# A start of its own for the first two batches: stacks copied inside SBUF, second-layer weights on other engines, an earlier output projection

## What is computed

```python
x = x + _L0_attn_ref(_layernorm(x), Wq, bq, Wk, bk, Wv, bv, Wo, bo)
x = x + _L0_ffn_ref(_layernorm(x), gamma, beta, fc1_q, fc1_scales, fc1_bias, fc2_q, fc2_scales, fc2_bias)
# attention: q = elu(x @ Wq.T + bq) + 1, k the same with Wk, v = x @ Wv.T + bv, in chunks of 128 tokens:
scores = where(mask, einsum('bqd,bkd->bqk', qi, ki), 0)
num = einsum('bqk,bkd->bqd', scores, vi) + einsum('bqd,bde->bqe', qi, S)
den = sum(qi * (cumsum(ki) + z)); out = num / den        # S += ki.T @ vi, z += sum(ki)
# then out @ Wo.T + bo
# feed-forward: w = (q - 128) * scales (groups of 128 rows), h = layernorm(x) * gamma + beta
y = silu(h @ w1 + fc1_bias); z = y @ w2 + fc2_bias; out = residual + 0.5 * z
```

## Time and profile before

| | |
|---|---|
| median of 3 runs | 1519.85 us |
| profiled execution | 1522.6 us |
| its span, first to last instruction | 1520.8 us |
| TensorE busy | 1493.2 us (98%) |
| VectorE busy | 1283.5 us (84%) |
| ScalarE busy | 1129.7 us (74%) |
| GpSimd busy | 680.7 us (45%) |
| mean granted TensorE clock | 0.991 |

### The profile page before, as it was taken

The page is one execution under the profiler, slowest core; times in us unless marked ns, Lnnn a source line. Parts: engine busy times, 40 slices in busy tenths (PEclk is TensorE's granted clock), DMA queues, the critical chain, the costliest instruction groups (busy, mean ns, idle before and its releaser), DMA issues.

```text
span 1520.8 us, 40737 instructions
## 1 busy us (share of the span) xinstructions
PE 1493.2 (98%) x14874; PEld 1311.2 (86%) x14874; DVE 1283.5 (84%) x2587; ACT 1129.7 (74%) x1917; POOL 680.7 (45%) x469
## 2 busy tenths in 40 slices
PE   7799999999999999999999999999999999999998
PEld 6588889888888888888888888888888888988887
DVE  6788888888888888888888888888888888888875
ACT  3487777887777887777887777887777877777863
POOL 3244344544344544345444445443445443445444
PEclk8899999999999999999999999999999999999999
DMA  7846765556765556764557765557654557755450
GB/s 198 194 118 150 179 148 149 137 131 152 179 158 131 131 133 164 179 156 133 131 122 175 179 133 143 137 125 179 179 138 138 133 129 179 174 134 141 117 127 28
DMA packets 153944, 222.96 MB, mean 147 GB/s; under 512 B 20032, under 2 KB 71488, under 8 KB 153920
## 3 DMA queue, kind: packets, MB, share of 16 engines
q1 hardware_dynamic: 152560, 222.63, 61.0%
q10 hardware_dynamic: 1360, 0.01, 0.1%
HBM read 138.69 MB, written 83.89 MB: 146 GB/s over the span
## 4 chain that ended last, share of the span: by engine, by line
PE 93%; DVE 2%; DMA 2%; POOL 1%; issue 1%; SPq 0%; ACT 0%; POOLq 0%; DVEq 0%
PE ring L342 35%; PE num L532 8%; PE ring L420 8%; PE sc L490 7%; PE ring L421 7%; PE sc L342 6%; PE num L499 4%; PE num L342 3%; PE state_acc L342 3%; PE ring L372 3%; PE state_acc L490 2%; PE ring L566 2%; PE state_acc L513 2%; PE num L421 1%; PE num L420 1%; PE num L372 1%
## 5 line engine op out<-in xcount | busy, mean ns | idle before, releaser
L1137 POOL TENSOR_TENSOR s_lo<-silu_f,s_hi 128x512 fp32r<-128x512 f32 x256 | 343.9, 1349 | 539.0 <-ACT s_hi L987 538.9
L342 PE MATMUL ring<-w_hi,s_hi 128*128 128x256 f32 x992 | 282.2, 284 | 0.0
L342 PE MATMUL ring<-w_lo,s_hi 128*128 128x256 f32 x992 | 278.9, 281 | 0.0
L342 PE MATMUL ring<-w_hi,s_lo 128*128 128x256 f32 x992 | 278.9, 281 | 0.0
L672 DVE TENSOR_TENSOR probs<-sc,causal 128x512 f32<-128x512 f32 x320 | 207.6, 681 | 16.1 <-PE sc L490 8.6
L342 PEld LDWEIGHTS ring<-w_hi,s_hi 128*128 128x128 f32 x992 | 187.8, 189 | 12.1 <-DVE phi_q L718 12.0
L1032 ACT ACTIVATE x_hat<-x,hn_add,ln_rstd 128x256 f32<-128x256 f32 x128 | 66.5, 590 | 174.6 <-DVE hn_add L860 174.6
L976 ACT ACTIVATE silu_f<-ring,bias,scale 128x512 f32<-128x512 f32 x217 | 167.5, 772 | 31.9 <-PE ring L421 23.5
L420 PE MATMUL ring<-gt_hi,w_q 128*128 128x512 f32 x441 | 190.5, 432 | 0.0
L342 PEld LDWEIGHTS ring<-w_hi,s_lo 128*128 128x128 f32 x992 | 188.0, 189 | 0.0
L342 PEld LDWEIGHTS ring<-w_lo,s_hi 128*128 128x128 f32 x992 | 187.9, 189 | 0.0
(11 more groups left out here) (204 smaller groups left out, 3946.2 us busy)
## 6 DMA issues: line engine op xcount, KB each, us to landing
k_stack<-k_rows SPq DMA_DIRECT2D x192, 256.0 KB, 4.1
q_stack<-q_rows SPq DMA_DIRECT2D x384, 128.0 KB, 6.2
k_rows<-silu_f SPq DMA_DIRECT2D x128, 256.0 KB, 2.6
q_rows<-probs SPq DMA_DIRECT2D x128, 256.0 KB, 2.5
x_in<-in_x SPq DMA_DIRECT2D x32, 512.0 KB, 8.4
xb<-in_x SPq DMA_DIRECT2D x32, 512.0 KB, 7.9
out<-clip SPq DMA_DIRECT2D x64, 256.0 KB, 7.5
silu_f<-in_q SPq DMA_DIRECT2D x2, 512.0 KB, 10.4
```

Source lines behind the costliest of these rows:

```text
L342: last = e.matmul(target, a, b, start=(n == 0), stop=(n == 3 * len(pairs) - 1))
L1137: sl.done(e.tensor_tensor(s_lo[:, j, :], silu_f[:, j % SLOTS, :], s_hi[:, j, :].bitcast(F32), ALU.subtract))
```

## The change

It touches the preparation and iterations 0 and 1, which is now unrolled as well (flag `second`); the loop begins at 2 and its order is as before.

- First stacks (batch 0): keys are copied from SBUF to SBUF by `first_keys`, 12 copies of 64 KB for each tile; SP issues those of tile 0, ScalarE those of tile 1. Queries still go over DRAM, those of tile 0 in two halves of the tokens. In iteration 0 SP does the same with the keys of tile 0 for batch 1 (`sp_second_stacks`), the others as before but in another order.
- Masked scores of batches 0 and 1 take the tiles in the order `FIRST_TILE`, which begins with the tiles that aren't `probs`.
- Second-layer weights: `fc2_q` is loaded at the start into x1 and res, the scales into `silu_f` once the key stacks are there; ScalarE casts, GpSimd multiplies and subtracts, ScalarE makes the high parts earlier.
- Iteration 0: TensorE does `output_projection` ahead of `project_kq(1)`; VectorE does `attention_sum` ahead of features(2) and features(3), and the small vectors' work (`ffn_preparation`) ahead of features(0); GpSimd adds `bias_o` and takes the power ahead of both products; it makes the low query part of tile 1.
- Iteration 1: TensorE does both `project_v`, `ffn_in`, the key transposes, fc1(0) to fc1(2) and the state update ahead of scores(0). VectorE starts with `ffn_input_lo` and the statistics of batch 2; GpSimd makes x_hat and the residual. ScalarE copies v before the FFN input.

```diff
-        w1_i = [flat(tile_[:, :, :]).bitcast(I32) for tile_ in (res, xb)]
-        w2_i = [by_group(flat(silu_f[:, 2 * n:2 * n + 2, :])).bitcast(I32) for n in range(2)]
-        sc2_b = [res, x1]
-        w2_f = [res, x_hat]
+        w1_i = [flat(silu_f[:, 2 * n:2 * n + 2, :]).bitcast(I32) for n in range(2)]
+        w2_f = [x1[:, :, :], res[:, :, :]]
+        w2_i = [ap.bitcast(I32) for ap in w2_f]
+        sc2_b = [by_group(flat(silu_f[:, 2 * n:2 * n + 2, :])) for n in range(2)]
...
+        FIRST_TILE = (3, 2, 0, 1, 3, 2, 0, 1)
...
 # TensorE, scores(u)
-                if c == 0:
+                if not Fn and c == 0 or second and u == 0:
+                    e.wait_ge(p_key_rows[t], 16 * 3 * PAIRS * (1 + Fn))
+                if not Fn and u == 0:
+                    e.wait_ge(p_query_rows, 16 * 6)
+                elif not Fn and u == 2:
+                    w.need(q_in[0], 0)
+                elif c == 0:
                     w.need(k_in[t], 0)
                     w.need(q_in[t], 0)
...
 # TensorE, order of iterations 1 and 0
+            if second:
+                project_v(0)
+                project_v(1)
+                ffn_in()
+                k_transposes(0)
+                k_transposes(1)
+                fc1(0)
+                fc1(1)
+                update_states()
+                fc1(2)
+                scores(0)
+                scores(1)
...
             project_kq(0)
-            project_kq(1)
+            if Fn:
+                project_kq(1)
             fc2(0)
             output_projection()
+            if not Fn:
+                project_kq(1)
...
 # VectorE
-                if u == 0:
+                if tile_of(u, Fn and not second) == 0:
+                    if not Fn:
+                        e.wait_ge(p_query_out, 16 * 2)
                     for t in range(T):
                         w.need(q_out[t], 0)
...
+            if second:
+                ffn_input_lo()
+                ve_norm_x(e, w, 1)
+                ffn_sum(0)
+                ffn_sum(1)
+                snapshots(0)
+                snapshots(1)
+                mask(0)
+                ffn_sum(2)
+                mask(1)
...
+            if not Fn:
+                attention_lo(1)
+                preparation[0]()
+                features(0, 1)
+                features(1, 1)
+                split_k_lo(0, 1)
+                split_lo(0, 1)
+                attention_sum()
+                features(2, 1)
+                features(3, 1)
+                norm_factors()
+                cumulate(0, 1)
+                split_k_lo(1, 1)
+                cumulate(1, 1)
+                return
...
 # ScalarE
+                if A and not Fn:
+                    e.wait_ge(p_w2_made, 2)
                 e_kh.done(e.activation(k_hi[:, t, :].bitcast(F32R), phi_k[:, t, :], ACT.Copy))
...
+            def weights_2_cast():
+                e.wait_ge(p_wdma["2"], 16 * 2)
+                for n in range(2):
+                    e.activation(w2_f[n], w2_i[n], ACT.Copy, bias=-128.0).then_inc(p_w2_cast, 1)
...
+            if not A and N:
+                w.need(e_kl, 1, 1)
+                for n in range(3):
+                    first_keys(e, 1, n)
...
 # GpSimd, iterations 0 and 1
+            if not Fn:
+                weights_2(0)
+                weights_2(1)
+                weights_2_lo(0)
+                input_bias()
+                norm_powers()
+                products(0)
+                split_q_lo(1)
+                products(1)
+                weights_2_lo(1)
+                return
+            if second:
+                po_norm(e, w, 1)
+                ffn_lo(0)
+                ffn_lo(1)
+                ffn_lo(2)
+                ffn_lo(3)
+                input_norm()
+                ffn_lo(4)
+                input_bias()
+                ffn_lo(5)
+                ffn_lo(6)
+                residual()
+                ffn_lo(7)
...
 # DMAs
+        def first_keys(e, t, n):
+            for g in range(PAIRS):
+                e.dma_start(k_stack[2 * HD * n:2 * HD * (n + 1), t, g, :].bitcast(F32),
+                            (k_hi, k_lo, k_hi)[n][2 * HD * g:2 * HD * (g + 1), t, :]).then_inc(p_key_rows[t], 16)
+        def sp_first_stacks(e, w):
...
+            w.need(e_kh, 1, 0)
+            first_keys(e, 0, 0)
+            w.need(e_ql, 1, 0)
+            queries_out(0, halves[0], p_query_out)
+            w.need(e_kl, 1, 0)
+            first_keys(e, 0, 1)
+            first_keys(e, 0, 2)
+            e.wait_ge(p_query_out, 16 * 2)
+            queries_in(0, halves[0], p_query_rows)
+            queries_out(0, halves[1], q_out[0].sem)
+            w.need(e_ql, 1, 1)
+            queries_out(1, whole, q_out[1].sem)
+            for t, toks in ((0, halves[1]), (1, whole)):
+                w.need(q_out[t], 1)
+                queries_in(t, toks, q_in[t].sem)
+        def sp_second_stacks(e, w):
...
+            w.need(e_ql, 1, 0)
+            queries_out(0)
+            w.need(e_kl, 1, 0)
+            for n in range(3):
+                first_keys(e, 0, n)
+            w.need(e_kl, 1, 1)
+            keys_out()
+            w.need(q_out[0], 1)
+            queries_in(0)
+            w.need(e_ql, 1, 1)
+            queries_out(1)
+            w.need(k_out[1], 1)
+            keys_in()
+            w.need(q_out[1], 1)
+            queries_in(1)
```

More of the change, by code:

```diff
@@ L771, in mask @@
                 for r in range(2):
-                    mask_half(e, w, u, r)
+                    mask_half(e, w, u, r, Fn and not second)
             def snapshots(t):
@@ L973, in ffn_scaled @@
                     w.need(sl, -1, j - SLOTS)
+                elif second and j % T == 0:
+                    e.wait_ge(p_key_rows[0], 16 * 3 * PAIRS * 2)
                 else:
@@ L1087, in ac_iteration @@
                 denominators_out()
+            if A and not Fn:
+                weights_2_cast()
             ffn_scaled(3)
@@ L1108, in ac_iteration @@
             ffn_silu(7)
+            if A and not Fn:
+                weights_2_hi(0)
+                attention_hi(1)
             if N:
@@ L1112, in ac_iteration @@
                 k_split_hi(0, 1)
-            if A:
+            if Fn and A:
                 attention_hi(1)
@@ L1116, in ac_iteration @@
                 q_split_hi(0, 1)
+                if A and not Fn:
+                    weights_2_hi(1)
                 exponentials(1, 1)
@@ new lines, in split_q_lo, with residual @@
+            def split_q_lo(t):
+                w.need(e_qh, 1, t)
+                w.need(av_pe, 0)
+                e_ql.done(e.tensor_tensor(q_lo[:, t, :].bitcast(F32R), phi_q[:, t, :], q_hi[:, t, :], ALU.subtract))
+            def residual():
+                w.need(res_c, -1)
+                e.wait_ge(p_w2_split, 2)
+                w.alone(e_out, -2)
+                for c in range(C):
+                    last = e.tensor_scalar(res[:, c, :], x1[:, c, :], res_mul[:, c:c + 1], res_add[:, c:c + 1],
+                                           ALU.mult, ALU.add)
+                res_m.done(last)
@@ new lines, in input_norm @@
+            def input_norm():
+                w.need(ln1_r, 1)
+                w.need(ht_pe, -1)
+                w.alone(xt_pe, 0)
+                for c in range(C):
+                    last = e.tensor_scalar(x_hat[:, c, :], x_in[:, c, :], mv1[:, c, 0:1], rstd1[:, c:c + 1],
+                                           ALU.subtract, ALU.mult)
+                xhat.done(last)
+            if not A and N:
+                products(0)
+                products(1)
+                po_norm(e, w, 2)
+                return
@@ new lines, in po_iteration @@
+            if not A:
+                for j in range(FT):
+                    ffn_lo(j)
+                    if j in (4, 5):
+                        w.need(res_m, -1)
+                        for c in (2 * j - 8, 2 * j - 7):
+                            last = e.tensor_tensor(res[:, c, :], res[:, c, :], bias_2[:, :], ALU.add)
+                        if j == 5:
+                            e_res.done(last)
+                return
+            if not Fn:
+                weights_2(0)
[3 more added lines that the diff above has]
+                norm_powers()
+                products(0)
+                split_q_lo(1)
+                products(1)
+                weights_2_lo(1)
+                return
@@ new lines, in po_iteration @@
+            if second:
+                po_norm(e, w, 1)
[3 more added lines that the diff above has]
+                ffn_lo(3)
+                input_norm()
+                ffn_lo(4)
+                input_bias()
+                ffn_lo(5)
+                ffn_lo(6)
+                residual()
+                ffn_lo(7)
+            else:
+                for j in range(FT):
+                    if j == FT - 2:
+                        input_bias()
+                    ffn_lo(j)
@@ L1165, in po_iteration @@
+            residual_bias()
+            if N:
+                products(0)
```

(14 more changed lines are left out.)

246 lines of the change are left out of this document (131 added, 115 removed).

## The result

The changed kernel takes 1524.62 us (median of 7 runs, 1523.54 to 1526.16) against 1520.24 us for the kernel before beside it (7 runs): a ratio of 1.0030, 95% interval 1.0018 to 1.0041. It is slower, by 0.3% or 4.4 us, where 8.1 us of gain were forecast: within 0.5% of no change, but above the range. The profiled execution took 1525.97 us, its span is 1524.1. A second set on another chip gave 1519.83 against 1515.94, ratio 1.0026 (1.0017 to 1.0035).

A forecast was written before the change was run, and what follows sets the result against it. TensorE, busy throughout 100 to 1400 us, bounds the kernel, so only the start of its continuous part can move. 8.4 us sooner less 0.3 for GpSimd gives 8.1: 1514.5 us profiled, 1511.7 median; range 1504 to 1518.5.

The forecast's parts named there:

- The output projection and the power sooner: Iteration 0, behind x1: factors at 65.3, 9.3 us sooner, and fc1(0) at 71.3 instead of 82.49.
- The second-layer weights on GpSimd: Iteration 0: scales land at 49, GpSimd's work on them ends at 58.6, ahead of x1 at 59.6.
- rival 2: Iteration 0: scales land at 53.3, GpSimd's weights make x1 3.3 us late; gain 4.8 us, 1515.1; chance 0.13.
- First stacks: the price of an issue: Batch 0: twenty issues at 0.46 us end at 28.0; scores(0) at 31.5, scores(4) at 44.3 instead of 46.30.
- Rival 1: Batch 0: DMA engines, not issues, set the stacks; scores(4) at 48.9; gain 3.5 us, 1516.3; chance 0.17.
- x1: the small vectors: Iteration 0: small vectors complete near 55.8, features(0) due at 56.8; x1 6.0 us after the key projections, at 59.6.
- scores(0): the queue: Second batch, SP's queue: eight issues, last at 70.8; queries land at 76.0, TensorE idle 1.2 us.
- To the anchor: Second batch, values(0) at 78.2 to its key projections (the anchor): 16.4 us plus 0.4, so 95.0, 8.4 us sooner.
- The third batch: x_hat on GpSimd: Iteration 1: GpSimd's x_hat and residual at 0.7 us an operation make fc2 late; 0.3 us charged.
- rival 3: Before the loop: copies land at the low ends and the clock stays up; gain 10.6 us, 1509.2; chance 0.10.
- rival 4: Iteration 1: GpSimd's one-input operations are slow; above 1.8 us each no gain, at 2.7 us 1527.5; chance 0.05.

The follow-up runs named there:

- the last of the first four experiments: The first experiment with the first batch's stacks over DRAM rows too: 1524.6 us, ratio 1.0020, 3.6 us over the first experiment on the same chip.
- The first experiment: The changed kernel with the second batch's stacks over DRAM rows again in the old order: 1520.99 us, ratio 0.9997 to the kernel before.
- the three edits: Changed kernel with second batch's stacks over DRAM, small vectors' work behind norm_factors, GpSimd's x_hat and residual ahead of its third low part: 1511.32 us, ratio 0.9978; again 1513.73 us.

## Why the prediction was wrong, step by step

Three steps of the sum failed. The queue ahead of the second batch's queries was priced as if the twelve key copies before them were over: scores(0) came at 82.61 and not at 76.0. The small vectors' work of VectorE was put at nothing: its first operation took 2.48 us. GpSimd's x_hat was put at 0.7 us an operation: it took 1.21. The largest is the first. The prediction's landmarks and those measured, with the length of each stretch:

| stretch | forecast, us | first profile, us | error | second profile, us |
|---|---|---|---|---|
| start to key projections of batch 0 | 53.6 | 54.70 | +1.1 | 55.06 |
| to x1 | 6.0 | 8.45 | +2.45 | 8.46 |
| to the factors | 5.7 | 5.29 | -0.4 | 5.29 |
| to fc1(0) | 6.0 | 5.68 | -0.3 | 5.68 |
| to scores(0) of the second batch | 4.7 | 8.49 | +3.8 | 7.48 |
| to the anchor | 19.0 | 22.44 | +3.4 | 21.76 |
| anchor to the third batch | 45.9 | 47.42 | +1.5 | 47.47 |

The errors of the first profile sum to 11.6 us, and 8.1 less 11.6 is its 3.5 us of loss.

**What held.** What bounds the kernel, and that the change can only move the start of the continuous part. The output projection and the power sooner: x1 to the factors and on to fc1(0) came out within 0.7 us. The second-layer weights on GpSimd: the scales had landed by 48.33, x1 didn't wait for them, so rival 2 fell. The first stacks as a gain: the last of the first four experiments takes 3.6 us back.

**First stacks: the price of an issue.** I took the 0.46 us of a load for every issue. The term was mis-sized: the copies inside SBUF cost 0.63 and more, the loads beside ScalarE's 0.60, so the twenty issues ended at 31.01 and not at 28.0. The landing behind them, 34.33 - 31.01 = 3.3 us, is near the 3.5 that I had. Scores(4) came at 46.03 instead of 44.3, and the stretch behind it gave 0.6 back. Rival 1 had scores(4) 4.6 us late, by a store of 7.84 us; it was 1.7 us late, and the stores landed in 2.7 and 3.4 us (medians), so it fell. A part of its mechanism is real: beside ScalarE's copies the loads take 1.2 us longer to land. (The stores' ends in that paragraph are slightly off too: the last of the four, issued at 29.3, lands at 31.8 or, with 7.84, at 37.2, not at 31.4 and 36. The 33 that I took lies between.)

**x1: the small vectors.** I checked when their data would be there, 55.8, and took their work as nothing. The data were there; the work was slow, beside GpSimd's addition. Moving it takes the stretch from 8.45 to 6.54 us, so 1.9 of the 2.45 us are this work. The other half microsecond is a slip in my sum: 4.5 us is the start of features(1), and I left out its own 0.75; with it the sum is 6.55. The trace of before had it at 0.28 us in a place of its own, and I moved the price with it. Here a page would have warned me: the Trainium skill, "SBUF — State Buffer", section "SBUF: two separate sides", says that VectorE and GpSimd share a pair of ports which is locked for a whole instruction, by a VectorE operation in a two-port mode or with two SBUF inputs (these against one of GpSimd that reads SBUF) or by one of GpSimd, whichever starts first, and that the other fully blocks. The trace agrees: 2.48 us with the end 0.15 behind GpSimd's, 0.28 alone; and 3.65 us for a low part with two SBUF inputs. The lock as such isn't measured here, only the lengthening.

**scores(0): the queue.** This is the step that failed most. I counted eight issues behind the key low part of tile 1 (two stores, six loads) and let them start at 67.6, as if the twelve key copies of tile 0 ahead of them were over by then. By my own times, from 60.4 and at 0.46 us each, they would have been, at 65.9; they began at 64.12, late by the first two errors, and took 8.81 us instead of 5.5 (7.80 in the second profile). So the stores went at 72.97 and the last load at 76.56, not at 70.8. It landed 5.92 us later, where I had 5.2. The wait became 4.39 us (2.72 in the second profile) where I had 1.2. The landing was nearly right and the queue wrong. The first experiment shows that the wait is this queue's: over DRAM, with 13 issues at the lower price instead of 22, it is gone.

**To the anchor.** The 16.4 us that I carried over had been at full clock. In the changed kernel the granted clock is 0.50 from 82 to 90. In the three edits, at full clock from 78 on, the stretch takes 98.83 - 78.53 = 20.3 us. So some 2.1 of the 3.4 us go with the lowered clock, and the rest was too low a figure of mine. The same window in the changed kernel, the first experiment and the three edits:

```profile
82.00:90.00 8.00, 6.61 (x39) 4.94 (x40) 4.10 (x7) 0.49 (x2) 0.53 (x1) 0.50 1.08 219
```

```profile
82.00:90.00 8.00, 7.94 (x74) 5.86 (x74) 5.19 (x10) 3.71 (x6) 2.11 (x2) 0.57 1.08 145
```

```profile
82.00:90.00 8.00, 6.90 (x83) 5.33 (x79) 5.89 (x11) 5.75 (x9) 8.00 (x10) 1.00 1.04 190
```

That the wait for the queries is what lowered the clock isn't shown. The first experiment doesn't have that wait, only the 1.19 and 1.11 us ahead of fc1(2) and scores(1), and its clock is as low and its stretch as long: 102.48 - 80.09 = 22.39 us. In the second profile of the three edits the clock falls too, to 0.79 in this window, and the stretch takes 20.75. I had put the clock under what may be gained and nowhere under what may be lost.

**The third batch: x_hat on GpSimd.** I had 0.7 us an operation; x_hat takes 4.84/4 = 1.21 and the residual 2.62/4 = 0.66. The faster rival 3 fell with the waits. This is the slower rival's mechanism, rival 4, at a size between my value and its point: 1.00 us of wait for s_lo, and 1.5 of period beyond the 0.3 that I charged. With the measured times, 4 x 1.21 and 4 x 0.66, the prediction's own sum for the two gives 1.4 us; the times were wrong, not the sum. That such work would run so fast that it costs nothing isn't borne out either: VectorE took 0.34 us for each of these operations in the kernel before (four in 1.37 and 1.38). (The point at which rival 4 is 7.6 us slower is p = 2.8, not 2.7.) Its place was a choice too: GpSimd had been idle 9.40 us right before, and there the same work is free. My sum began with the order as given and followed it to the end, without asking whether the slack lay on the other side.

**What stays open.** Single edits are worth 4.4 to 5.0, 3.0 to 3.6 and 2.7 to 3.3 us, 10 to 12 in sum; together they are worth 6.1 us by the medians on one chip and up to 7.9 by the ratios. With 2 us either way on each of these, it isn't shown whether they overlap. Even with the three edits the kernel gains 2.2 to 3.7 us and not 8.1: its anchor is at 98.83 and not at 95.0, by the dearer first issues (1.2), the slip at x1 (0.5), a later fc1(0) and scores(0) (1.2 together) and the figure to the anchor, which was 1.3 too low. Why the loads are issued more slowly beside ScalarE's copies wasn't tried.

## What to carry to other kernels

Where a transfer is cut into many small ones, price the issuing queue first, with the row of that very kind of copy if there is one: twelve issues of 0.65 to 0.73 us held back six loads whose bytes the DMA engines could have moved. Before an operation goes to GpSimd or to another time, look at what runs on VectorE and GpSimd beside it there, and put GpSimd's new work into the gap that the trace shows rather than where its result is due. A longer wait on TensorE can cost more than its length: with all stacks over DRAM, scores(4) came 1.0 us later and the key projections 4.9, at the lowered clock. But where something else is late in that stretch, as at fc1(0), a higher clock gave nothing back.

## What the runs showed of the hardware

- Issuing a copy of 64 KB from SBUF to SBUF took SP 0.63 to 0.73 us (four in 2.52, twelve in 7.79 to 8.81) and ScalarE 0.64 (twelve in 7.68). Issuing a load from DRAM rows took 0.46 to 0.51 for 128 KB (six in 2.76 to 3.03), and for 64 KB 0.49 alone and 0.60 beside ScalarE's issues.
- A VectorE operation of 128x256 took 2.48 us beside an operation of GpSimd and 0.28 alone; one of 128x512 with two SBUF inputs took 3.65, where that form takes 1.11 on the mean of 64, and the same with one input from PSUM 0.68. A running sum of 128x512 took 2.30 beside two operations of GpSimd and 1.22 alone.
- GpSimd's two-step operation (a product and a sum or difference with one number a partition) of 128x256 took 1.21 us for x_hat and 0.66 for the residual, which have the same shape. In the gap they took 1.21 again (four in 4.84) and 0.54 (four in 2.16); VectorE took 0.34 for either. The reason is open.
- The granted clock in the same place differed between two executions of one program: 0.50 and 1.00 from 70 to 74 us.
